# A megakernel's attention stage: its instruction order planned with durations instead of ticks, and a DMA transpose for three of four batches

## The reference

```python
xn = layernorm(x)                                   # no weights
q, k, v = (xn @ W.T + b, split into 16 heads of 32) # three projections
scores = q @ k.T / sqrt(32); causal -> -inf; scores += -slope[h] * |i - j|
attn = softmax(scores) @ v ;  attn = attn @ Wo.T + bo
probs = softmax(xn @ gate_w.T); the two best experts, weights to sum 1
expert(e) = (silu(xn @ w1g[e].T) * (xn @ w1u[e].T)) @ w2[e].T
out = x + attn + weighted sum of the two experts
```

## Time and profile before

| | |
|---|---|
| median of 3 runs | 1599.39 us |
| the profiled execution itself | 1597.73 us |
| its span, first to last instruction | 1595.9 us |
| mean granted PE clock | 0.952 |
| PE busy | 1419.4 us (89%) |
| DVE, ACT, POOL busy | 947.9, 799.1, 948.4 us |
| first score to last score of the attention (L1271) | 74.28 to 1117.5 us |

### The profile page before, as it was taken

One profiled execution on the slowest core, in us unless ns is written; L12 is line 12 of the kernel. 1 busy time (PEld: TensorE's weight loads), 2 busy tenths in 40 slices (PEclk: granted clock), 3 DMA queues, 4 the chain that ended last, 5 costly groups with the idle time before them and its releaser, 6 DMA issues.

```text
span 1595.9 us, 32893 instructions
## 1 busy us (share of the span) xinstructions
PE 1419.4 (89%) x12219; PEld 838.9 (53%) x12219; DVE 947.9 (59%) x1742; ACT 799.1 (50%) x1403; POOL 948.4 (59%) x756
## 2 busy tenths in 40 slices
PE   4689978989997999998899899877789999999995
PEld 2355545544554555555455456543356656566663
DVE  8567776666687657766669976672243333333332
ACT  5255666646677675766676455456122222222221
POOL 4134576645577655656675567676217777777774
PEclk9899998989999999998899999997899999999998
DMA  6245433435533536333244210233877778888973
GB/s 245 61 128 148 124 94 102 123 90 148 156 94 97 152 101 197 103 117 94 88 110 126 83 43 13 68 115 106 288 180 126 136 130 131 131 137 148 132 137 47
DMA packets 189156, 193.51 MB, mean 121 GB/s; under 512 B 104883, under 2 KB 138931, under 8 KB 188876
## 3 DMA queue, kind: packets, MB, share of 16 engines
q1 hardware_dynamic: 160492, 152.01, 35.7%
q0 software_dynamic: 26128, 37.24, 13.9%
q10 hardware_dynamic: 2384, 2.16, 0.4%
HBM read 92.88 MB, written 53.74 MB: 92 GB/s over the span
## 4 chain that ended last, share of the span: by engine, by line
PE 55%; DVE 13%; POOL 11%; DMA 7%; issue 6%; ACT 4%; SPq 4%; ACTq 0%; POOLq 0%; DVEq 0%
PE S L1359 15%; PE O L1390 4%; PE M L1390 4%; DVE arena L1643 4%; PE T L1210 3%; DVE arena L1656 3%; DMA arena<-arena 3%; PE M L1289 3%; PE S L1210 3%; PE S L1243 2%; SPq L1059 2%; PE T L1243 2%; PE S L1271 2%; PE O L1289 2%; POOL arena L2006 2%
## 5 line engine op out<-in xcount | busy, mean ns | idle before, releaser
L1875 ACT ACTIVATE arena<-S,psl 128x512 f32<-128x512 f32 (+1 forms) x640 | 399.5, 641 | 256.0 <-PE S L1273 152.2
L2064 POOL DMA_INDIRECT out<-arena x142 | 222.1, 1564 | 104.7 <-issue 40.5
L1359 PE MATMUL S<-arena 128*128 x1704 | 267.1, 313 | 5.2 <-issue 5.2
L1643 DVE TENSOR_REDUCE arena<-S 128x1 f32<-128x512 f32 (+3 forms) x311 | 202.0, 655 | 113.5 <-PE S L1248 82.4
L1643 DVE TENSOR_REDUCE arena<-T 128x1 f32<-128x512 f32 (+3 forms) x297 | 193.0, 654 | 95.5 <-PE T L1248 65.3
L1359 PEld LDWEIGHTS S<-arena 128*128 128x128 f16 x1704 | 166.8, 98 | 102.3 <-issue 5.8
L1271 PE MATMUL S<-arena 106*128 106x256 f16 x640 | 182.0, 285 | 40.7 <-ACT arena L1875 39.2
L1999 POOL TENSOR_TENSOR arena<-arena 128x512 f32<-128x512 f32 (+1 forms) x64 | 135.7, 2121 | 81.5 <-ACT arena L1875 81.4
L1984 POOL TENSOR_TENSOR arena<-arena 128x512 f16<-128x512 f32 x64 | 79.9, 1250 | 165.2 <-ACT arena L1832 165.0
L1763 DVE COPY arena<-T 128x512 f16<-128x512 f16 x71 | 30.1, 425 | 218.4 <-PE T L1374 215.4
L2006 POOL TENSOR_TENSOR arena<-arena 128x1024 f32<-128x1024 f32 x48 | 114.8, 2392 | 75.4 <-ACT arena L1875 46.9
(11 more groups left out here) (216 smaller groups left out, 2679.4 us busy)
## 6 DMA issues: line engine op xcount, KB each, us to landing
arena<-arena SPq DMA_DIRECT2D x192, 128.0 KB, 3.0
arena<-in_w1T SPq DMA_DIRECT2D x64, 352.0 KB, 3.6
arena<-in_x SPq DMA_DIRECT2D x64, 256.0 KB, 4.2
w_d<-arena SPq DMA_DIRECT2D x32, 352.0 KB, 2.8
arena<-w_d SPq DMA_DIRECT2D x16, 704.0 KB, 6.2
arena<-in_w2T SPq DMA_DIRECT2D x32, 256.0 KB, 3.0
out<-arena SPq DMA_DIRECT2D x32, 256.0 KB, 3.6
xn_d<-arena SPq DMA_DIRECT2D x24, 256.0 KB, 2.8
```

The costliest lines, as they stand in the source:

```text
L1359: tp = pe.matmul(y[:, i * 512:i * 512 + I], xT[:, s % XDEEP, 4 * a + c, :], weights[:, bass.ds(reg[s] + (w_ * NX * W1N + c * 2 * I + i * I ...
L1643: dve.tensor_reduce(d[:, heads[0]:heads[-1] + 1], z, AX, ALU.max).then_inc(sems["mx"], 1)
L1875: act.activation(PT[t % 3][:, h, 0:n], CB[o.bank["score", u]][:, 0:n], ACT.Exp, scale=psl[:, hh:hh + 1]).then_inc(sems["exp"], 1)
L2064: pool.indirect_dma_start(out=halves, out_offset=bass.IndirectOffsetOnAxis(row[:, part, s:s + 1].bitcast(U32), 0), in_=yo[:, s % YDEEP, c0 ...
```

## The change

Two things are changed.

**The order of the attention.** The tick loop and its generators go (`maxima`, `score`, `products`, `sums`, `emptied`, `o_load`, `proj_o`, `w_max`, `w_split`, `routing`, `first_slots`, `ln_steps` and others). In their place every step of the stage is declared once, with its engine, a cost in us, a due value in units, and the steps that it follows. `Steps.run` plays the engines through: an engine that is free takes, among the first open steps of its lines, the ready one with the smallest due value; if none is ready it waits for the next event. The order in which steps are taken becomes the list. Costs are constants such as 0.22 and 0.28 for a score, 0.63 and 0.52 for an exp, 2.35 and 2.8 for an add, 0.87 for a third of a projection; a DMA step holds SP for its issue and is done 3.0 to 4.2 us later. Every semaphore wait in the engine programs stays, but for those of the second thing. Everything up to tick -9 and the whole expert stage are ordered as before.

**The transpose.** For batches 1 to 3, `xtp` and the ACT copy `xt` go. A DMA transpose on SP's queue, right behind the store `xnd`, writes the tile from its place into `xnT`. It waits for the last v projection of the batch before. The place is free when both DMAs have landed.

```diff
+ADD_DUE, ACC_DUE, PV_DUE, RS_DUE = 3, 3.5, 3.2, 6.2
+PRE_DUE, PRE_STEP, MTR_DUE = -27, 1.05, 3.0
+FILL0, FILL1, TURN0, TURN1, STACK_DUE = 4, 38, 6, 44, 0
+LN0, LN_STEP, GATE0 = 55, 18, 120
+O_DUE = (-20, -8, 4, 24)
+MAX_STEP, SPLIT0, SPLIT_STEP = 2.2, 150, 7.4
+DMA_LAG = 4.2
+LAG = {"PE": 0.1, "ACT": 0.06, "DVE": 0.08, "POOL": 0.08, "SP": DMA_LAG}
...
+    def run(self, start, pace, last):
...
+                best = None
+                for k, line in enumerate(lines[e]):
+                    s = line[at[e][k]]
+                    if best is not None and s.due >= best[0]:
+                        continue
+                    if s.since is not None and s.since > now:
+                        continue
+                    if s.lock and held not in (None, s.lock[0]):
+                        continue
+                    if s.take and len(o.owner) == len(o.since):
+                        continue
...
+                    best = s.due, k, s
...
+                o.add(*s.key, sem=s.sem, inc=s.inc)
+                free[e] = t + cost
+                done[s.key] = t + cost + (LAG[e] if s.lag is None else s.lag)
...
+    for u in range(NU):
+        new("PE", 0.22 if i < q else 0.28, u, "score", u,
+            follows=[("exp", u - 2), ("stack", b, g, h), ("mrow", G, q)])
+        new("ACT", 0.63 if i < q else 0.52, u + 0.4, "exp", u, follows=[("score", u), ("pv", t - 3), ("add", t - 3)])
...
+        new("POOL", (2.2 if q == 0 else 2.35) if i == 0 else 2.35 if i < q else 2.8, u + ADD_DUE, "add", t,
+            follows=[("exp", u), *before])
+        new("ACT", 0.54, d + 0.8, "osb", G, q, follows=[("rsum", t), ("aT", *divmod(4 * G + q - 2, 4))])
...
+                new("DVE", 0.83, d, "xn", b, half, i, follows=[("newton", b, half)])
+                new("SP", 0.6, d + 3, "xnd", b, half, i, inc=16, follows=[("xnl", b, half, i)], lag=3.0)
+                new("SP", 0.9, d + 3.5, "xt", b, half, i, inc=16, lag=4.2,
+                    follows=[("xnl", b, half, i), ("v", b - 1, NG - 1, 1, 3)])
...
-    u = U0
-    while u < NU or fill or pace or events or later:
-        now[0] = u
-        flush()
-        if 0 <= u < NU:
-            score(u)
-        for f in events.pop(u, []):
-            f()
...
-        credit = min(credit + 0.62, 1.0)
...
+    w.run(U0, PACE, NU - 1)
...
+            elif kind == "xt" and key[0]:
+                on.wait_ge(*at("xnl", b, half, i))
+                on.wait_ge(*at("v", b - 1, NG - 1, 1, 3))
+                sp.dma_start_transpose(xnT[:, :, :, tt * P:(tt + 1) * P].rearrange("p a c n -> p (a c) n"),
+                                       XH[half_place(b, half, i)]).then_inc(at(*step)[0], 16)
...
-                    on.wait_ge(*at("xtp", *half_before(*key)))
-                    on.wait_ge(*at("xnd", *half_before(*key)))
+                    stored_and_turned(on, *half_before(*key))
```

More of the change, by code:

```diff
@@ L206, in ln_turn @@
         later.append(rest)
[L208 to L222, removed]
     def proj_qk(b, g, qk, half):
@@ L341, in sums @@
[L341 to L360, removed]
-                o.give(("bc", G, q), ("a32", G, q))
-                at(now[0] + 1, lambda: add("aTh", G, q))
-                at(now[0] + 2, lambda: add("aT", G, q))
-                ready["aT", G, q] = now[0] + 4
-            later.append(rest)
-        at(now[0] + 4, inverse)
-        at(now[0] + 9, spread)
@@ new lines, in plan @@
+    for b in range(1, B):
+        norm(b)
+    for b in range(B):
+        d = 10 if b == 0 else 160 * (b - 1) + GATE0
+        if b == 0:
+            new("ACT", 0.3, 4, "gwh", since=3)
+            new("DVE", 0.95, 4.5, "gwl", follows=[("gwh",)])
+        for part in range(4):
+            key = "gate", b
+            new("PE", 0.7, d + 2 * part, *key, part, take=key if part == 0 else None, lock=(key, part == 3), inc=part == 3,
+                follows=[("xt", b, 1, 3), ("gwl",)])
+        new("DVE", 0.22, d + 8, "lg", b, follows=[("gate", b, 3)], give=(key, ("lg", b)))
@@ new lines, in plan @@
+    for part in range(2):
+        key = "gmax", "o", part
+        new("PE", 0.1, U0 + 2 + 2 * part, *key, take=key, follows=[("gtop", "o", 0)] if part else [])
+        new("DVE", 0.5 if part == 0 else 0.1, U0 + 3 + 2 * part, "gtop", "o", part, follows=[key], give=(key, ("gtop", "o", part)))
+    new("DVE", 0.9, U0 + 5.5, "scales", 2, follows=[("gtop", "o", 1)])
+    for i in range(2):
+        new("ACT", 1.07, U0 + 6 + 2 * i, "woh", i, follows=[("scales", 2)])
+        new("DVE", 1.2, U0 + 7 + 2 * i, "wol", i, follows=[("woh", i)])
@@ L729, in plan @@
-    o.ended, o.forced = u, forced
+                d, step = at_ + O_DUE[k] + 3 * (i % 2), 0.8
+            key = "o", b, i
+            for third in range(3):
+                new("PE", 0.87, d + step * third, *key, third, take=key if third == 0 else None, lock=(key, third == 2),
+                    inc=third == 2, line="o", since=NU - 1 if b == B - 1 else None,
+                    follows=[("aT", b * NG + g, k) for g in range(NG)] + [("wol", 1)])
+            new("DVE", 0.7, d + step * 3, "y", b, i, follows=[(*key, 2), ("xbo", b, i)], give=(key, ("y", b, i)))
@@ new lines, in plan @@
+    route(0.95, (0, 0), inc=1)
+    new("ACT", 0.4, d[0] - 1.5, "rex", follows=[("route", 0, 0)])
+    route(1.4, (1, 0), follows=[("rex",)])
+    for i in range(0, NT, 8):
+        route(0.9, (2, i))
+    for i in range(0, NT, 4):
+        route(0.55, (6, i))
+    route(1.4, (10, 0))
+    route(1.1, (11, 0))
+    route(1.5, (11, 1), inc=1)
+    new("PE", 0.9, d[0] - 1.5, "rank", take=("rank",), follows=[("route", 11, 1)])
+    route(0.85, (12, 0), inc=1, follows=[("rank",)])
+    w.all["route", 12, 0].give = ("rank",), ("route", 12, 0)
@@ L731, in up @@
+    for k, (u, n) in enumerate(((603, 10), (622, 4), (NU, 6), (NU, 6), (NU, 2))):
+        new("SP", 0.6 * n, u, "win", k, inc=0, since=u, follows=before + more[k], lag=0.0)
+    w.run(U0, PACE, NU - 1)
     def up(s):
```

572 lines of the change are left out of this document (285 added, 287 removed).

## The result

The changed kernel takes 1510.12 us (median of 4 runs, 1507.14 to 1517.76) against 1601.39 us for the kernel before on the same chips (4 runs, 1597.41 to 1604.67). The ratio is 0.9438, 95% interval 0.9396 to 0.9481: 91 us less. The profiled execution took 1509.31 us with a span of 1507.5. Two executions further down, one of run 1 (2038 us) and one of run 11 (2372 us), had a granted clock of 0.66 and 0.56 throughout, and the ratios leave them out.

What follows compares the result with a forecast made beforehand. PE was taken to bound the attention. Terms 27 (idle, first 14 groups) + 20 (clock) + 4 (last two groups) + 15 (transposes) = 66 us off 1597.7, giving 1531.7, as median 1533 us; forecast range 1505 to 1557, chance 0.46.

Steps and rivals of the forecast that it cites:

- What bounds: Attention, 1044 us: PE, busy 934, sets its end; only less PE work, less PE idling or a higher clock counts.
- Idle time of the first 14 groups and of the last two, 27 + 4 us: Attention groups: the new order returns 27 us of PE idle time in the first 14, 4 in the last two.
- I take half: First 14 groups: half the upper end, 54 us idle and 40 clock, because the planner replays constants for varying durations.
- The clock, 20 us: First 14 groups: PE's granted clock follows its idle time; half of 40 us of clock loss comes back.
- The transposes, 15 us: Turns between batches: 24 tiles lose eight PE transposes each, 0.62 us a tile; 15 us, lower end 10.
- The late turn: Rival: transposes through three places delay next-batch projections, 10 to 24 us over three turns; 1557 to 1591 us, chance 0.17.
- row maxima fill the gap: Turns: argument against the late-turn rival, that row maxima of the next group can fill PE's missing work.
- quiet everywhere: Rival: all groups like 5, 7 and 13, half the last groups' loss goes; 128 us, 1471 us, chance 0.15.
- The constants miss: Rival: tight order stalls on varying durations in layer-norm, routing or weight-piece groups; slower, 1634 or 1709 us, chance 0.15.
- What would show it: Profile signs: attention 977 us, PE idle 79, clock near 0.97, `score` waits under 20, no turn idle over 4.
- The three waits behind `osb`: Turns: `osb`, heading ACT's queue, waits for `aT` and delays an exp; PE idles 4.29 us, once per turn.

Runs made afterwards that it cites:

- run 1: Changed kernel with the planned order alone, batches 1 to 3 turned by PE transposes and ACT copies as before: 1507.77 us, ratio 0.9401.
- run 11: Kernel before, ordered by ticks, with `osb` and the chain behind it put down two ticks later: 1621.1 us, ratio 1.0116.
- run 3: Changed kernel with one cost per engine for every step in the planner: 1569.54 us, ratio 0.9789.
- run 4: Changed kernel with each step's planner cost times 0.7, 1.0 or 1.3 by a fixed draw on its name: 1537.15 us, ratio 0.959.
- run 8: Planned order, weight maxima on PE and DVE, PE transposes with seven eighths left out for batches 1 to 3, ACT copies full size: 1501.72 us, ratio 0.9378.
- run 7: Changed kernel with PE transposes and ACT copies for all batches and POOL's all-reduce replaced by PE and DVE steps: 1500.67 us, ratio 0.9374.
- run 9: Changed kernel with the all-reduce replaced by PE and DVE steps and the DMA transpose's issue declared at 1.3 us, not 0.9: 1496.46 us, ratio 0.9345.
- run 2: Kernel before, still ordered by ticks, with DMA transposes for batches 1 to 3: 1623.82 us, ratio 1.0134.
- run 5: Changed kernel with POOL's all-reduce of the weight maxima declared at 13 us instead of 0.5 in the planner: 1502.03 us, ratio 0.937.
- run 6: Changed kernel with POOL's all-reduce replaced by a PE transpose, a DVE maximum and a product with ones: 1495.21 us, ratio 0.9321.
- run 10: Kernel before, ordered by ticks, with `aT` put down one tick earlier: 1604.48 us, ratio 1.0016.
- run 12: Changed kernel with eight expert-weight loads held back until the last block's fold has landed: 1510.98 us, ratio 0.9419.

## Why the prediction was right, and where it was not

The direction, the stage and the main cause (idle time made by the order, and the clock with it) were right. The time was 23 us too high, and one of four terms was wrong.

- **What bounds.** Right. All of the gain is in the attention; start, tail and experts together moved 8.4 us, which is work moved forward.
- **Idle time of the first 14 groups and of the last two, 27 + 4 us.** Measured 109.9 - 57.3 = 52.6 us. The last two gave 25.6 - 12.2 = 13.4 us, the upper end of what I had, the others 39.2 of the 54 (84.3 - 14 x 2.1 is rather 55). For the order alone run 1 is the measure: there the first 14 groups idle 34.4 us, 50 less than before. "I take half" was the step that failed in size; the order took nearly all. Runs 3 and 4 give the scale: with one cost per engine the order gives 33 us, with errors of 30% 64, with its own 91.
- **The clock, 20 us.** By the same sum as in the prediction it was 52.3 us and is 0.01 x 946.4 = 9.5: 43 us, again about the upper end. It followed the idle time, as I had said, and more than in proportion: PE idles half as long, and its slow clock is down to a fifth. But that sum claims too much: it takes all time at the lower level as work that would go in half of it, and a single `score` product took 0.39 us at that level and 0.27 at the higher (the same product at 221.39 us). PE's busy time is a closer measure: it fell by 933.3 - 889.1 = 44.2 us in the attention. Of these 8.8 are now done ahead of the first score, and 11.5 are the transposes by run 1, which leaves some 24 us for the clock. That is an estimate, since the 8.8 and the 11.5 hold some change of clock themselves. With the 52.6 us of idle time it adds up to the 96.8 us of the attention, and it is near the 20 that I took.
- **The transposes, 15 us.** Wrong. "PE, the bounding engine" was true of the stage and not of the turn. Run 1 has the whole gain without them, run 8 takes 168 PE transposes away for nothing, and the surest pair (runs 7 and 9) gives 4 us. PE idles in the turns whatever is taken off it: groups 2, 6 and 10 together idle 18.1 us in the changed kernel, 10.7 in run 1 and 11.9 in run 8.
- **The late turn.** Its mechanism is real, and its size fits in part: 10 to 24 us were said, with three places and a landing up to 9.7 us. In run 2 the three turn groups idle 13.1 us more, each first projection comes 9.4, 6.5 and 3.1 us later, and PE waits up to 4.3 us for a transpose there. The run's 22 us are more than that, and the rest is not explained. Under the planned order the first of the three gaps shrank to 15.6 us and the others are 18.0 and 17.3, about as under the order by ticks. Compared with PE transposes in the same order (run 1) the second and third come 6 to 7 us later. That this costs little fits what I had named against the rival, that row maxima fill the gap; no run tests it.
- **The rivals.** The measured 1510 us lie between "quiet everywhere" (1471) and the forecast (1533). Quiet everywhere fails by groups 2, 3, 6, 10 and 12, which idle 4.7 to 9.4 us. "The constants miss" did not happen by the chip's variation, but run 4 shows the mechanism: 27 us for errors of 30%, inserted. The one constant that missed by far, 0.5 us for 13 us of POOL, cost 8 us by the medians and 3.7 in the attention (run 5), and the step itself another 7, or 5.8 in the attention (run 6).
- **What would show it.** I had said 977 us of attention, 79 us of idle time, a clock near 0.97, `score` waiting under 20 us and no idle stretch of PE over 4 us in a turn. It was 946, 57, 0.99 and 15.0; in the turns the longest is 2.1 us. The longest of all, 6.5 us, lies outside the turns, in group 3, where I had looked for nothing. The three waits behind `osb` are gone, but no run shows that they were worth what they seemed: run 10 did not remove them, and run 11 can't tell.

## What to carry to other kernels

Where several in-order engines share a stage and PE idles only in some of its parts, plan the order by playing it through with measured durations: in run 1 that took 94 of 1602 us with the same instructions, and up to two thirds of it hang on the declared durations, so measure them and look for the one that is off by more than ten times. Before moving work off the busiest engine, look whether it is busy at that place: here 12 us of PE work were all but free in the turn, and replacing them by DMAs made the kernel 22 us slower under the old order. And a lone POOL step of a rare kind is worth a look at the idle time around it, in which nothing is named.

## What the runs showed of the hardware

- One all-reduce over the partitions kept POOL from other work for 5.90 + 0.37 + 6.61 = 12.9 us, and 5.63 + 0.37 us and up to 7.31 behind in the kernel before. Without it the attention was 9.5 us shorter (run 6).
- In run 6 the granted clock is 1.00 in 10 of the 16 groups, 0.97 or 0.98 in five and 0.88 in the last. The six are groups in which PE idles 2.3 us or more, but three others with 2.8, 3.2 and 4.6 us stay at 1.00. In run 2 it is 0.83 to 0.86 in the three groups in which PE idles 14 to 17 us.
- The DMA transposes of a 256 KB tile inside the attention held SP 1.33 us and landed in 3.8 us at the median, 3.1 to 4.9; between loads and stacks one took 6.9 us. In the tail a 4 KB fold took 10.9 us beside eight large loads on another queue, and at most 4.5 us without them (run 12); a 256 KB store behind the same loads took 12.9.
